# Tables of two expert layers stored partition by partition, the last sums made in the mix's block, and the norms applied by ScalarE

## The reference

```python
def _layernorm(x, axis=-1, eps=1e-05):
    m = jnp.mean(x, axis=axis, keepdims=True)
    v = jnp.var(x, axis=axis, keepdims=True)
    return (x - m) / jnp.sqrt(v + eps)

h = _L0_tok_ref(x, ...)                          # 16 of every 128 rows
h = h + _L0_attn_ref(_layernorm(h, axis=-1), ...)  # retention
h = h + _L0_ffn_ref(_layernorm(h, axis=-1), ...)   # expert layer 1: 8 experts, best one of them
h = h + _L1_attn_ref(_layernorm(h, axis=-1), ...)  # cross attention to 128 x 64 video rows
h = h + _L1_ffn_ref(_layernorm(h, axis=-1), ...)   # expert layer 2: best two of 8
```

## Time and profile before

| | |
|---|---|
| time, median of 3 runs | 2454.87 us (2453.16 to 2456.1) |
| profiled execution | 2457.68 us |
| its span in the profile | 2455.9 us |
| outside the span | 1.8 us |
| PE busy | 2150.6 us (88%) |
| DVE busy | 1985.9 us (81%) |
| ACT busy | 1689.1 us (69%) |
| POOL busy | 1446.6 us (59%) |
| cross attention | some 1600 us, 65% of the span |

### The profile page before, as it was taken

One profiled execution on the slowest core, in us unless ns is written; L12 is line 12 of the kernel. 1 busy time (PEld: TensorE's weight loads), 2 busy tenths in 40 slices (PEclk: granted clock), 3 DMA queues, 4 the chain that ended last, 5 costly groups with the idle time before them and its releaser, 6 DMA issues. The chain is left out here.

```text
span 2455.9 us, 49808 instructions
## 1 busy us (share of the span) xinstructions
PE 2150.6 (88%) x14597; PEld 1692.2 (69%) x14597; DVE 1985.9 (81%) x3132; ACT 1689.1 (69%) x4826; POOL 1446.6 (59%) x1416
## 2 busy tenths in 40 slices
PE   4566876838999999999999999999999999967883
PEld 3345766825777777777777777777777777757883
DVE  6977764147999999999999999999999999866664
ACT  1154212516888888888888888888888888803662
POOL 2643433754666666666666666666666666623773
PEclk9675666968999999999999999999999999967997
DMA  7421023622222222222222222222222222143655
GB/s 242 142 69 44 28 60 94 168 60 61 65 64 65 65 64 64 65 64 64 65 64 64 65 64 64 65 64 64 65 65 64 64 65 64 43 96 101 156 154 154
DMA packets 157683, 197.68 MB, mean 80 GB/s; under 512 B 33200, under 2 KB 99888, under 8 KB 155504
## 3 DMA queue, kind: packets, MB, share of 16 engines
q1 hardware_dynamic: 139280, 174.80, 26.5%
q0 software_dynamic: 8064, 16.60, 2.5%
q10 hardware_dynamic: 10208, 4.66, 0.7%
HBM read 77.58 MB, written 17.74 MB: 39 GB/s over the span
## 5 line engine op out<-in xcount | busy, mean ns | idle before, releaser
L1945 POOL TENSOR_TENSOR attend_weights<-attend_weights,attend_scales 128x512 f32<-128x512 f32 x1024 | 1036.3, 1043 | 560.6 <-DVE attend_scales L1862 560.6
L1840 DVE TENSOR_REDUCE attend_maxima<-attend_psL 128x16 fp32r<-128x1024 f32 x512 | 624.5, 1220 | 89.5 <-PE attend_psL L1755 89.5
L1856 DVE TENSOR_REDUCE attend_sums<-attend_weights 128x16 f32<-128x1024 f32 x512 | 619.0, 1209 | 0.1
L1908 ACT ACTIVATE attend_turned<-attend_psT 128x512 f32<-128x512 f32 x1024 | 554.4, 596 | 9.0 <-PE attend_psT L1774 5.9
L1774 PE MATMUL attend_psT<-consts,attend_weights 128*128 128x128 f32 x4096 | 530.8, 272 | 0.8 <-POOL attend_weights L1945 0.8
L1774 PEld LDWEIGHTS attend_psT<-consts,attend_weights 128*128 128x128 f32 x4096 | 477.5, 140 | 66.1 <-POOL attend_weights L1945 1.3
L1788 PE MATMUL attend_psA<-attend_turned,attend_value_ring 128*64 128x256 f32 x4096 | 498.5, 385 | 0.8 <-ACT attend_turned L1908 0.8
L1901 ACT ACTIVATE attend_weights<-attend_psL,attend_maxima 128x64 f32<-128x64 f32 x2048 | 446.6, 329 | 53.1 <-DVE attend_maxima L1840 53.1
L1754 PE MATMUL attend_psL<-attend_key_ring,attend_q_high 128*128 128x512 f32 x1024 | 430.6, 420 | 1.6 <-ACT attend_q_high L1886 1.6
L1755 PE MATMUL attend_psL<-attend_key_ring,attend_q_low 128*128 128x512 f32 x1024 | 404.1, 395 | 0.0
L1788 PEld LDWEIGHTS attend_psA<-attend_turned,attend_value_ring 128*64 128x64 f32 x4096 | 271.5, 136 | 154.4 <-issue 43.7
(11 more groups left out here) (316 smaller groups left out, 2368.8 us busy)
## 6 DMA issues: line engine op xcount, KB each, us to landing
attend_key_ring<-keys SPq DMA_DIRECT2D x512, 128.0 KB, 2.2
attend_value_ring<-values SPq DMA_DIRECT2D x128, 256.0 KB, 2.5
moe2mix_w_tile<-in_L_ffn_w_dram SPq DMA_DIRECT2D x71, 256.0 KB
select_xbuf<-in_x_dram SPq DMA_DIRECT2D x16, 1024.0 KB, 5.4
moe1mix_w_tile<-in_L_ffn_W_dram SPq DMA_DIRECT2D x39, 256.0 KB, 3.1
select_emb<-L_attn_video_embeds_dram ACTq DMA_DIRECT2D x16, 256.0 KB, 4.3
values_gates<-project_vg SPq DMA_DIRECT2D x8, 512.0 KB, 2.6
retain_vg<-values_gates SPq DMA_DIRECT2D x8, 512.0 KB
```

The lines of the kernel that those rows point to most:

```text
L1840: dve.tensor_reduce(maxima[:, both, :].rearrange("p j v -> p (j v)"), psL[:, both, :].rearrange("p j (v f) -> p (j v) f", f=FR), X, ALU.ma ...
L1856: dve.tensor_reduce(sums[:, both, :].rearrange("p j v -> p (j v)"), weights[:, both, :].rearrange("p j (v f) -> p (j v) f", f=FR), X, ALU. ...
L1908: act.activation(turned[:, parity, :, h, t, :], psT[:, j % 2, :].rearrange("p (k q) -> p k q", k=SUB), ACT.Copy).then_inc(turned_copied, 1)
L1945: pool.tensor_tensor(w, w, scales[:, s, :, None].to_broadcast([P, VC, FR]), ALU.mult).then_inc(normalised, 1)
```

## The change

- `normed_dram` and `result_dram` are seen as "(p g) d -> p g d": row g of partition p lies at p * 32 + g. The constant `token1` becomes `place1` with that number, so `source` and `target` point there. `token`, unused, goes. Each partition's part in one DMA is now one piece: 4 KB (4160 B for layer 2's table) in `normed_dram` and in the last read-back, 2 KB in the cross norm's. The rows of one gather or scatter lie over the whole table of 2 MB instead of near each other.
- `add_back` goes as a block. Its DMAs stand at the end of SP's program in the mix's block of layer 2, behind a wait for all scatters, its additions at the end of DVE's.
- The norm of both routings and of the cross attention is split: DVE does `statistics` (with a `shift` = -mean * root, two batches behind), ACT does `apply`, four activations of 128 x 128 with scale and bias per partition. The norm ahead of the projection keeps `batches`.
- In the cross norm the additions of the read-back rows move from POOL to DVE, one batch ahead of the statistics. ACT's loop there is written out.
- In layer 2's mix the DVE steps of `finish` count on the same semaphore as those of `begin`.

```diff
-        "token1": np.arange(G)[None, :] * P + p[:, None] + 1.0,
+        "place1": p[:, None] * G + np.arange(G)[None, :] + 1.0,
...
+    def statistics(self, dve, hidden, before=None):
+
+        for b in range(B + 2):
+            if b < B:
+                if before:
+                    before(b)
+                for g in range(b * TB, (b + 1) * TB):
+                    dve.bn_stats(self.stats[:, g, :], hidden[:, g, :]).then_inc(self.steps, 1)
+            if b > 1:
+                part = slice((b - 2) * TB, (b - 1) * TB)
+                dve.wait_ge(self.root_ready, b - 1)
+                dve.scalar_tensor_tensor(self.shift[:, part], self.mv[:, part, 0], -1.0, self.root[:, part], ALU.mult, ALU.mult).then_inc(self.shift_ready, 1)
+            if b < B:
...
+                    dve.bn_aggr(self.mv[:, g, :], self.stats[:, g, :]).then_inc(self.steps, 1)
+                dve.wait_ge(self.steps, (b + 1) * 2 * TB)
+                dve.tensor_scalar(self.square[:, part], self.mv[:, part, 1], self.scale, self.eps, ALU.mult, ALU.add).then_inc(self.square_ready, 1)
+
+    def apply(self, act, hidden, rows, ready, b):
+
+        act.wait_ge(self.shift_ready, b + 1)
+        for g in range(b * TB, (b + 1) * TB):
+            ins = act.activation(rows[:, g, 0:D], hidden[:, g, :], ACT.Identity, bias=self.shift[:, g:g + 1], scale=self.root[:, g:g + 1])
+        ins.then_inc(ready, 1)
...
-                    table = K.normed_dram[top].rearrange("(g p) d -> p g d", p=P)
+                    table = K.normed_dram[top].rearrange("(p g) d -> p g d", p=P)
...
                     act.nop().then_inc(normT_copied, 2)
+                    norm.apply(act, K.hidden, normed, norm_ready, 0)
                     for b in range(B):
+                        if b + 1 < B:
+                            norm.apply(act, K.hidden, normed, norm_ready, b + 1)
                         act.wait_ge(normT_ready, b + 1)
...
-                    norm.batches(dve, K.hidden, normed, norm_ready)
+                    norm.statistics(dve, K.hidden)
...
+                    if last:
+                        for n in range(RING):
+                            sp.wait_ge(result_out[n], 16 * len(range(n, used, RING)))
+                        for q in range(PARTS):
+                            part = slice(q * QT, (q + 1) * QT)
+                            for k in range(2):
+                                tokens = K.result_dram[2][SPARE + k * N:SPARE + (k + 1) * N, :].rearrange("(p g) d -> p g d", p=P)
+                                sp.dma_start(back[:, k, part, :], tokens[:, part, :]).then_inc(back_in[q], 16)
+                        rows_out = out.rearrange("b (i p) d -> p (b i) d", p=P)
+                        for q in range(PARTS):
+                            part = slice(q * QT, (q + 1) * QT)
+
+                            sp.wait_ge(added, 2 * (q + 1))
+                            sp.dma_start(rows_out[:, part, :], K.hidden[:, part, :]).then_inc(stored, 16)
+                        sp.wait_ge(stored, 16 * PARTS)
...
-        if last:
-            add_back(nc, K, phase, out)
...
                 def _(dve):
-                    def landed(b):
+                    def add_rows(b):
+                        part = slice(b * TB, (b + 1) * TB)
+                        dve.wait_ge(back_in[b], 16)
+                        dve.tensor_tensor(K.hidden[:, part, :], K.hidden[:, part, :], back[:, part, :], ALU.add).then_inc(rows_added, 1)
+
+                    def added(b):
+                        if b == 0:
+                            add_rows(0)
+                        if b + 1 < B:
+                            add_rows(b + 1)
                         dve.wait_ge(rows_added, b + 1)
...
-                    norm.batches(dve, K.hidden, rows, norm_ready, before=landed)
+                    norm.statistics(dve, K.hidden, added)
```

More of the change, by code:

```diff
@@ L1474, in _ @@
                 def _(dve):
-                    steps, later = Steps(dve, mix_steps), Steps(dve, finish_steps)
+                    steps = Steps(dve, mix_steps)
                     def of_expert(table, e):
@@ L1502, in finish @@
                         dve.wait_ge(root_ready, t + 1)
-                        later.mark(dve.reciprocal(inverse[:, r:r + 1], root[:, r:r + 1]))
-                        later.then(dve.scalar_tensor_tensor(res, res, mv[:, r, 0:1], of_expert(gamma, e), ALU.subtract, ALU.mult))
+                        steps.mark(dve.reciprocal(inverse[:, r:r + 1], root[:, r:r + 1]))
+                        steps.then(dve.scalar_tensor_tensor(res, res, mv[:, r, 0:1], of_expert(gamma, e), ALU.subtract, ALU.mult))
                         dve.scalar_tensor_tensor(res, res, inverse[:, r:r + 1], of_expert(beta, e), ALU.mult, ALU.add).then_inc(scaled, 1)
@@ L1515, in _ @@
                             finish(t - FINISH_AT, owners[t - FINISH_AT])
[L1518 to L1553 removed]
+                    if last:
+                        for q in range(PARTS):
+                            part = slice(q * QT, (q + 1) * QT)
+                            dve.wait_ge(back_in[q], 32)
+                            for k in range(2):
+                                rows_q = K.hidden[:, part, :]
+                                dve.tensor_tensor(rows_q, rows_q, back[:, k, part, :], ALU.add).then_inc(added, 1)
+                                dve.wait_ge(added, q * 2 + k + 1)
 def cross_attention(nc, a, K):
@@ L1641, in _ @@
                     act.nop().then_inc(normT_copied, 2)
-                    with act.Fori(0, B // 2) as it:
-                        for s in range(2):
-                            b = it * 2 + s
-                            act.wait_ge(normT_ready, b + 1)
-                            act.activation(qT[:, ds(b * L, L)], psT[:, s, :], ACT.Copy).then_inc(normT_copied, 1)
+                    norm.apply(act, K.hidden, rows, norm_ready, 0)
+                    for b in range(B):
+                        if b + 1 < B:
+                            norm.apply(act, K.hidden, rows, norm_ready, b + 1)
+                        act.wait_ge(normT_ready, b + 1)
+                        act.activation(qT[:, b * L:(b + 1) * L], psT[:, b % 2, :], ACT.Copy).then_inc(normT_copied, 1)
         with ExitStack() as inner:
```

43 lines of the change are left out of this document (14 added, 29 removed).

## The result

| | before | changed |
|---|---|---|
| time, median of 7 runs | 2456.1 us (2451.28 to 2461.32) | 2439.84 us (2436.15 to 2445.58) |
| span of the profiled execution | 2455.9 us | 2434.3 us |
| PE, DVE busy | 2150.6, 1985.9 us | 2145.1, 1960.2 us |
| ACT, POOL busy | 1689.1, 1446.6 us | 1723.5, 1437.7 us |

The changed kernel takes 0.9935 of the time before (95% interval 0.9918 to 0.9952), 16 us less.

The account below looks back on a forecast made before the run. Bounds seen: a DVE-POOL ring with PE close in routings, DVE-POOL blocking in the cross norm, POOL in layer 2's mix, full DMA at the end. 0 + 6.9 + 0 + 7.4 = 14.3 off 2454.87: 2440.6; range 2434 to 2448.

Parts of the forecast that it names:

- Routings: Both routings: PE becomes the bound at 2.55 us a round, a later start cancels the gain; 0 each.
- rival 5: Routings: PE's clock rises to 2.4 GHz once its idle time goes; 9.6 us less, 2431; chance 0.06.
- The start: Routing 1: shift 0 waits for the third statistics; first turn at 361.1 instead of 359.29, turn 2 at 365.5.
- Cross norm: Cross attention's norm: additions on DVE and apply on ACT make rounds of 2.4 us; 6.9 us less.
- rival 3: Cross norm: POOL's root goes first, so each DVE addition waits; 6.2 us given back, 2446.8; chance 0.11.
- Block: Program's end: without the block change the first read leaves at 2429.4 instead of 2432.97; 3.6 us less.
- Transfers at the end: Last read-back: 4 KB pieces move at 401 GB/s instead of 278; 3.8 us less.
- the queue: Program's end: three stores issued during the reads wait behind them, then take 4.6 us; the fourth 1.5 more.
- The start and the rate: Last read-back: 1.6 us from issue to data, then 4.19 MB at 401 GB/s in 10.5 us.
- Gathers and scatters: Both mixes: spread row addresses cost nothing, slower landing being hidden; 0, bounds 1 faster and 4 slower.
- Rival 6: Mixes: spread rows slow the gathers beyond their slack; 19 us more at a landing of 13.0, 2460; chance 0.05.
- rival 2: Last read-back: piece size brings nothing, the end gains only the block's 3.6; 10.5 in all, 2444.4; chance 0.13.

Follow-up runs that it names:

- experiment 8: Changed kernel with the norm applied by DVE again in both routings, on a slower chip (before 2524.36 to 2526.53 us): 2510.34 us, routings 27.3 each.
- experiment 5: Changed kernel with the cross norm's apply back on DVE, additions staying on DVE, on a slower chip (before 2524.36 to 2526.53): 2512.2 us, cross norm 28.7.
- experiment 6: Changed kernel with the cross norm's additions back on POOL, apply staying on ACT, on a slower chip (before 2524.36 to 2526.53): 2511.87 us, cross norm 25.7.
- experiment 12: Changed kernel with the cross norm's read-back issued in layer 1's mix block and each shift one batch behind, after the square: 2436.11 us, 0.9913 of before.
- experiment 7: Changed kernel with a DVE memset ahead of six cross-norm additions, on a slower chip (before 2524.36 to 2526.53): 2512.57 us, cross norm 26.0.
- experiment 3: Changed kernel with the last sums in a block of their own again, on a slower chip (before 2524.36 to 2526.53): 2515.64 us.
- experiment 2: Changed kernel with DRAM rows ordered by group again (512 B pieces), on a slower chip (before 2524.36 to 2526.53): 2506.78 us, read to end 22.9.
- experiment 1: Changed kernel unaltered, in five rounds beside the kernel before, on a slower chip: 2507.44 us, 0.993 of before.
- experiment 4: Changed kernel with last reads, additions and stores in halves (8 KB pieces), on a slower chip (before 2524.36 to 2526.53): 2508.76 us, read to end 21.9.

## Why the prediction was right

2440.6 was forecast, from a median of 2454.87, and 2439.84 came, beside a median of 2456.1. 14.3 us were forecast and 16 measured, 17.1 by the stretches. That the two times lie within 0.8 us of each other is partly luck: the median before moved up by 1.2 meanwhile, and one term that was too large stands against three that were too small. The mechanism of each part held, except that in the cross norm the bound passed from DVE to ACT.

- *Routings, 0 forecast, 1.2 and 1.1 measured* (experiment 8). The bound was the right engine: PE without idle time, clock 0.50, and rival 5 is out. The start was mis-sized. Shift 0 was put 4.14 behind the first statistics and ended at 3.64. In turn, an applied batch takes 1.64, not 1.26: eight take 3.18 and four 1.64, a pitch of 0.39, not the 0.26 of those that read PSUM. The first turn came at 5.38 (5.54 forecast), but turn 2, from which PE sets the pace, at 9.18 (361.19) instead of 9.94: 0.76 of the gain. The rest is the round: 2.45 for five rounds (361.19 to 373.46), as a turn's loads take 0.90, not 0.72, but begin 0.26 before those of the product have ended (362.08 + 1.83 against 363.65); summing the two groups of before gave 2.55.
- *Cross norm, 6.9 forecast, 8.0 measured* (experiments 5 and 6). DVE's round was mis-sized: 2.4 forecast, 2.00 measured. 0.16 was a wait of the shift for the root that can't occur with the shift two behind: the shift in round b needs the root of round b - 2. The other 0.25 came from adding durations: the next instruction starts 0.60 behind the addition's start (0.68 put), and the shift lies in a pause that is there anyway, 0.90 from the last statistics to the aggregates with it and 0.90 without it (experiment 12; 1.07 put). With DVE faster, ACT (2.02; 1.9 forecast) bounds instead: DVE's last shift comes 17.3 behind the first addition, 2.9 earlier than forecast, and ACT leaves 1.1 of it. That the addition goes first, keeps its 0.68 and the root gives the time was as forecast, so rival 3 doesn't occur in this kernel. What a root does that has begun first stays open (experiment 7).
- *Block, 3.6 forecast, 4.1 measured* (experiment 3). The first read leaves 2.40 behind the last scatter's issue, not 2.9: the last scatter's landing and the wait together take less than the median landing of 2.6 plus 0.3.
- *Transfers at the end, 3.8 forecast, 2.8 measured* (experiment 2). That larger pieces move faster held, and so did the queue: in the trace's DMA records the first store, issued at 2421.84, moves its first 512 B piece at 2426.55, when the 4 KB pieces of the reads are nearly through (the last at 2427.52). The start and the rate were mis-sized. Additions of the kernel before, and the changed kernel's reads before any store moves:

```profile
2438.96 2.48 DVE L1552 TENSOR_TENSOR hidden<-hidden,moe2back_back 128x1024 f32<-128x1024 f32 x2 [14.12 <-DMA moe2back_back<-result]
2442.62 2.49 DVE L1552 TENSOR_TENSOR hidden<-hidden,moe2back_back 128x1024 f32<-128x1024 f32 x2 [1.18 <-DMA moe2back_back<-result]
```
```profile
2418.00:2420.00 2.00, 0.00 (x0) 0.00 (x0) 0.67 (x1) 0.00 (x0) 0.00 (x0) 0.50 0.98 371
2420.00:2422.00 2.00, 0.00 (x0) 0.00 (x0) 1.78 (x2) 0.00 (x0) 0.00 (x0) 0.50 1.03 408
```

  The first pair lands 5.17 behind the first read, where 1.6 and a quarter at 401 GB/s made 4.2. That is 0.95 of the 1.7 by which the last pair was too late. The 1.6 was wrong already for the kernel before: its first pair came after 5.99 and the second 3.66 later, a quarter at 287 GB/s, so some 2.3 lay ahead of the data. The next two quarters arrive in 5.47 us, 383 GB/s, not 401: 0.24. The last takes 3.19 us, 329 GB/s: 0.57. It is slow while no store's data moves; the rate falls to 221 GB/s from 2425 to 2426, and in experiment 1 to 225 in the same quarter, but not with 8 KB pieces, where no store is issued ahead of the reads' end (experiment 4). What causes the fall isn't shown. The last pair lands 13.8 behind the first read instead of 12.1; what follows is 6.3 instead of 7.0.
- *Gathers and scatters, 0 forecast and 0 measured.* Mixes 98.5 and 191.0, against 98.5 and 191.6 with rows near each other. Rival 6 is out.

The Trainium skill (DMA: Bandwidth & Descriptors, "Specifications") has 512 B as enough for line rate; here 512 B pieces read at 278 to 291 GB/s, 4 KB at 360 over 10 us and 8 KB at 414 to 434, so for this transfer the measurement decides against it, and rival 2 with it. The exclusive lock that the Trainium skill (SBUF — State Buffer, "SBUF: two separate sides") describes is seen in experiment 6, where a large addition on POOL holds up a 128 x 4 operation of DVE; the same section of the Trainium skill lets whichever starts first keep the ports until it ends. Against that stands DVE's shift, with two inputs in SBUF, which runs inside a root at 355.51 in its usual 0.14 while the root keeps its 1.01. Experiment 7, where the root starts first by the records and the addition isn't held up, doesn't decide on it, as the memset stands ahead of both.

## What to carry to other kernels

When an operation moves from one engine to another, recount the round of each engine and find the next bound by its own rows: here DVE fell from 3.68 to 2.00 and ACT, at 2.02, took over unnoticed. Sum rounds from start to start, not from durations, since queued instructions overlap here by up to 0.09 us. A transfer that nothing but a block boundary holds back is worth issuing ahead of it: 4.1 us here at the end of the program, and 2.3 or more in its middle.

## What the runs showed of the hardware

- POOL's large addition (128x512) stops a 128x4 operation of DVE (0.17 to 1.04 us). In the changed kernel it is the root that grows beside DVE's addition, from 1.01 to 1.38, and behind a memset and an addition to 1.73 (experiment 7). It ends 0.86 to 0.87 behind the addition's end in both.
- DRAM to SBUF by size of piece: 278 to 291 GB/s at 512 B, 360 over 10 us at 4 KB (371 to 408 in its best 4 us), 414 to 434 at 8 KB.
- Stores of SyncE that were issued while its reads were under way moved their first data 4.7 us later (5.2 in experiment 1), when the reads were nearly through.
- The same kernel's mixes take 98 and 191 us on one chip and 120 and 236 on another. The kernel before has no profile there, but its time is 68 us longer too. What causes it isn't shown.
- Retention's last part, untouched, takes 132.2 to 132.7 or 134.9 to 136.8 us from kernel to kernel, and the first read of the cross norm reaches DVE in 2.7 to 3.0 or 4.9 to 5.2. Differences of whole spans of two profiles hold such steps, so the stretches were compared instead.
